# A float32 second product in column groups for a short last row block, in a mixture-of-experts kernel on one core

## The reference

```
top1 = argmax(softmax(x @ router_w + router_b))
for i in range(8):
    h = x @ w1[i] + b1[i]                 # 256 -> 2048
    a, g = split(h, 2)                    # 1024 each
    y = (a * sigmoid(g)) @ w2[i] + b2[i]  # 1024 -> 256
    out = out + where(top1 == i, y, 0)
out = x + out
```

## Time and profile before

| | us |
|---|---|
| median of 3 runs | 217.95 |
| profiled execution, time | 217.55 |
| profiled execution, span | 215.8 |
| prologue, to PE's first matmul of tile 0 | 38.8 |
| tiles 0 to 7 and the end | 177.0 |

### The profile page before, as it was taken

How to read it: one execution, slowest core, us unless ns; L and a number is a source line. 1 busy time by engine, 2 the same in 40 slices (tenths; PEclk the granted TensorE clock), 3 DMA queues, 4 the chain that set the end, 5 groups by cost and what they waited for, 6 DMA issues and landing times.

```text
span 215.8 us, 4313 instructions
## 1 busy us (share of the span) xinstructions
PE 205.6 (95%) x1500; PEld 191.2 (89%) x1502; DVE 159.1 (74%) x307; ACT 121.8 (56%) x204; POOL 124.6 (58%) x146
## 2 busy tenths in 40 slices
PE   6986998899999999999999999999999999999992
PEld 3756843799999999999999999999999999999991
DVE  6826984877835999298969879994898469874960
ACT  2333692365916666386684958483949185745620
POOL 5000038776730788558878787887487818730751
PEclk9999999999999999999999999999999999999998
DMA  4995523799757173976499559837835692720011
GB/s 140 368 402 186 219 82 91 257 274 380 220 131 307 46 234 71 314 196 204 109 289 288 186 114 362 295 91 184 355 114 180 178 313 70 248 49 0 24 39 36
DMA packets 16964, 41.26 MB, mean 191 GB/s; under 512 B 2856, under 2 KB 11177, under 8 KB 14762
## 3 DMA queue, kind: packets, MB, share of 16 engines
q1 hardware_dynamic: 11490, 28.32, 36.7%
q0 software_dynamic: 4512, 10.50, 19.4%
q10 hardware_dynamic: 936, 2.17, 2.6%
HBM read 36.78 MB, written 6.03 MB: 198 GB/s over the span
## 4 chain that ended last, share of the span: by engine, by line
PE 67%; POOL 14%; issue 8%; DVE 5%; DMA 3%; ACT 1%; DVEq 0%; ACTq 0%; POOLq 0%
PE y_ps L1049 7%; PE y_ps L1051 7%; PE y_ps L1050 7%; PE g_ps L1029 5%; PE g_ps L1034 5%; PE g_ps L1030 5%; POOL out_dram L384 5%; PE a_ps L1029 5%; PE a_ps L1034 5%; PE a_ps L1030 5%; POOL y_out L375 5%; PE y_ps L870 3%; PE y_ps L875 3%; DMA xg<-x_rows,g_idx 3%; POOL xg L363 3%
## 5 line engine op out<-in xcount | busy, mean ns | idle before, releaser
L384 POOL DMA_INDIRECT out_dram<-y_out,s_idx x30 | 44.0, 1466 | 41.2 <-DVE y_out L793 30.4
L524 ACT ACTIVATE arena<-g_ps,b_t 128x384 f32<-128x384 f32 (+1 forms) x64 | 34.4, 538 | 48.2 <-PE g_ps L1034 48.2
L766 DVE SCALAR_TENSOR_TENSOR arena<-a_ps,b_t,arena 128x384 f32<-128x384 f32 (+1 forms) x64 | 36.0, 563 | 30.9 <-PE a_ps L1034 28.4
L363 POOL DMA_INDIRECT xg<-x_rows,g_idx x32 | 37.1, 1159 | 37.1 <-DVE g_idx L732 26.5
L1049 PE MATMUL y_ps<-w_hi,u_hi 128*128 128x256 f32 x168 | 48.5, 289 | 0.1
L1050 PE MATMUL y_ps<-w_lo,u_hi 128*128 128x256 f32 x168 | 47.5, 283 | 0.0
L1051 PE MATMUL y_ps<-w_hi,u_lo 128*128 128x256 f32 x168 | 47.5, 283 | 0.0
L375 POOL DMA_INDIRECT y_out<-in_x_dram,g_idx x32 | 40.3, 1259 | 9.8 <-issue 9.8
L665 DVE TENSOR_TENSOR w_lo<-w_raw,w_hi 128x1024 fp32r<-128x1024 f32 x32 | 37.3, 1221 | 4.7 <-DMA xg<-x_rows,g_idx 3.0
L530 ACT ACTIVATE u_hi<-arena 128x384 fp32r<-128x384 f32 (+1 forms) x64 | 30.7, 480 | 16.0 <-DVE arena L766 16.0
L1029 PE MATMUL g_ps<-xr_hi,w_hi 128*128 128x256 f32 (+3 forms) x128 | 37.0, 303 | 0.6 <-ACT xr_hi L512 0.6
(11 more groups left out here) (150 smaller groups left out, 298.3 us busy)
## 6 DMA issues: line engine op xcount, KB each, us to landing
w_raw<-in_L_ffn_w_dram SPq DMA_DIRECT2D x16, 1024.0 KB, 8.9
w_raw<-in_L_ffn_w_dram SPq DMA_DIRECT2D x16, 512.0 KB, 5.0
arena<-in_x_dram SPq DMA_DIRECT2D x4, 512.0 KB, 6.2
x_rows<-arena ACTq DMA_DIRECT2D x4, 512.0 KB, 3.0
b_all<-in_L_ffn_b_dram SPq DMA_DIRECT2D x1, 1024.0 KB, 4.9
xg<-x_rows,g_idx POOLq DMA_INDIRECT x32, 7.1
y_out<-in_x_dram,g_idx POOLq DMA_INDIRECT x32, 4.5
out_dram<-y_out,s_idx POOLq DMA_INDIRECT x30
```

Source lines behind the costliest of these rows:

```text
L363: nc.gpsimd.indirect_dma_start(out=xg[:, s * DIM:(s + 1) * DIM], out_offset=None, in_=x_rows, in_offset=bass.IndirectOffsetOnAxis(ap=g_idx ...
L384: nc.gpsimd.indirect_dma_start(out=out_flat, out_offset=bass.IndirectOffsetOnAxis(ap=s_idx[:, i * NSUB + s:i * NSUB + s + 1], axis=0), in_ ...
L524: nc.scalar.activation(sig[:, c % SIG_RING, 0:n], pair[c % RING][1][:, 0:n], ACT.Sigmoid, bias=b1_t[:, bass.ds(e * (2 * NC) + (NC + c), 1) ...
L766: V.scalar_tensor_tensor(u32[:, c % (8 - SIG_RING), 0:n], pair[c % RING][0][:, 0:n], b1_t[:, bass.ds(e * (2 * NC) + c, 1)], sig[:, c % SIG ...
```

## The change

**PE.** For the sizes 192, 288 and 320 (`PARTS`: a last block of 32 or 64 tokens) the last block is computed by the new `part_block`: plain float32 matmuls from unsplit u (`u32`) and unsplit w2 (`w2_whole`), 64 or 32 columns of the array for one chunk, so that two or four chunks stand side by side in column groups that write to different partitions of `y_ps[1]`. Each group accumulates its own chunks. It waits for `pair_free` of each chunk and for `w2_whole`, in place of `u_lo`.

**DVE.** `add_parts` adds the partial sums of the groups above the first to the output rows: one addition of 64 partitions for 192 and 320, three of 32 for 288, in branches on the control word of the tile before.

**Widths.** The sizes are now 192, 256, 288, 320, 352, 512 (384 is gone, 192 is new; PE's first product still has at least 256 columns). ACT and DVE use widths of 256, 288, 320, 384 or 512 (`if_width`), a chain of branches over five bodies.

**Memory and loads.** `u32` holds all eight chunks and lies in `x_t`, which is free after the prologue. `w2_whole` takes the half of `arena` that `u32` had. SP loads it, 1 MB for each tile, after the next tile's w1 and when the second product of the tile before has ended.

With the given inputs tiles 0 (64 tokens over), 2 (64), 4 (32), 5 (32) and 7 (64) get a `part_block`; DVE's and ACT's widths fall from 384 to 320 in tile 0 and from 384 to 288 in tiles 4 and 5.

```diff
-    SIZES = (256, 288, 320, 352, 384, 512)
+    SIZES = (192, 256, 288, 320, 352, 512)
+    PARTS = {size: (size // P, size % P) for size in SIZES if size % P in (32, 64)}
...
+        def if_width(eng, word, body, low=0):
+            widths = (2 * P, 288, 320, 3 * P, ITEM)
+            firsts = (0, SIZES.index(288), SIZES.index(320), SIZES.index(352), SIZES.index(ITEM))
+            if low == len(widths) - 1:
+                body(widths[low])
+                return
+            with eng.If(f_size(word) < firsts[low + 1]):
+                body(widths[low])
+            with eng.Else():
+                if_width(eng, word, body, low + 1)
...
+            def load_w2_whole(e):
+                if e > 0:
+                    sp.wait_ge(w2_whole_loaded, 16 * e)
+                    sp.wait_ge(mm2_done, e)
+                sp.dma_start(w2_whole, w2[e].rearrange("(c p) d -> p c d", p=P)).then_inc(w2_whole_loaded, 16)
...
+            def add_parts(i, word, sizes_here):
+                def of_sizes(left):
+                    if not left:
+                        dve.sem_inc(dve_chain, more)
+                        return
+                    s, wide = PARTS[left[0]]
+                    with dve.If(f_size(word) == SIZES.index(left[0])):
+                        rows = y_out[i % YB][0:wide, s * DIM:(s + 1) * DIM]
+                        for g in range(1, P // wide):
+                            link(V.tensor_tensor(rows, y_ps[1][g * wide:(g + 1) * wide, PLACE[s] * DIM:(PLACE[s] + 1) * DIM],
+                                                 rows, ALU.add))
...
+                    with dve.Else():
+                        count[0] = start
+                        of_sizes(left[1:])
...
+            def part_block(size, at1, at2, at16, done=None):
+                s, wide = PARTS[size]
+                groups = P // wide
+                pe.wait_ge(w2_whole_loaded, at16)
+                for c in range(NC):
+                    pe.wait_ge(pair_free[c], at2 if c >= CARRIED else at1)
+                    g = c % groups
+                    last = T.matmul(y_ps[1][g * wide:(g + 1) * wide, PLACE[s] * DIM:(PLACE[s] + 1) * DIM],
+                                    u32[:, c, s * P:s * P + wide], w2_whole[:, c],
+                                    start=c < groups, stop=c >= NC - groups)
```

More of the change, by code:

```diff
@@ L261, in if_blocks, with word_registers @@
                     body(4)
+        def if_width(eng, word, body, low=0):
[8 more added lines that the diff above has]
+                if_width(eng, word, body, low + 1)
+        def word_registers(eng):
+            return [eng.alloc_register(f"word_at{a}") for a in range(2)]
         def word_register(eng, name):
@@ L552, in _ @@
             for e in range(NE):
[L553 removed]
+                if_width(act, this_word(act, word_at), lambda n: gate_tile(e, e, n))
             for i in range(NE, TAB):
@@ L785, in bank_rows, with add_rows, add_last @@
                 return rows[:, 1:3] if h else rows[:, 0:4:3]
-            def add_rows(i):
+            def add_parts(i, word, sizes_here):
[9 more added lines that the diff above has]
+                                                 rows, ALU.add))
+                        if P // wide - 1 < more:
+                            dve.sem_inc(dve_chain, more + 1 - P // wide)
+                    with dve.Else():
+                        count[0] = start
+                        of_sizes(left[1:])
+                start = count[0]
+                more = max(P // wide for _, wide in PARTS.values()) - 1
+                of_sizes(sizes_here)
+                count[0] = start + more
+            def add_rows(i, word):
                 dve.wait_ge(mm2_done, i + 1)
                 dve.wait_ge(b2_added, i + 1)
[L791 to L796, removed]
+                half = bank_rows(i, 0)
+                V.tensor_tensor(half, y_ps[0][:, :].rearrange("p (s d) -> p s d", s=2), half, ALU.add)\
+                    .then_inc(y_done[0], 1)
+                half = bank_rows(i, 1)
+                link(V.tensor_tensor(half, y_ps[1][:, :].rearrange("p (s d) -> p s d", s=2), half, ALU.add))
+                if word is not None:
+                    add_parts(i, word, list(PARTS))
+                dve.sem_inc(y_done[1], 1)
+            def add_last(i, blocks, n, word):
                 dve.wait_ge(b2_added, i + 1)
@@ L809, in add_last, with gate_tile @@
                     dve.sem_inc(y_done[h], 1)
-            def gate_tile(i, e, blocks):
-                n = blocks * P
+            def gate_tile(i, e, n, word=None, word_before=None, chain_at=None):
+                if chain_at is not None:
+                    count[0] = chain_at
+                blocks = -(-n // P)
                 split_x(i, n)
@@ L834, in gate_tile @@
                 if i == NE - 1:
-                    add_last(i, blocks)
+                    add_last(i, blocks, n, word)
             dve.wait_ge(x_rows_written, 4 * 16)
```

71 lines of the change are left out of this document (48 added, 23 removed).

## The result

The changed kernel takes **235.5 us** (median of 4, 232.3 to 237.4) where the kernel before takes 218.1; the ratio of the undisturbed runs is **1.069 (1.054 to 1.085)**. A second measurement gave 237.6 against 217.9, ratio 1.085 (1.078 to 1.092). The forecast was 224.4 (217.6 to 228.3): the direction was right, the size 11 us too small and outside the range.

The account below looks back on a forecast made before the run. PE, busy in 95% of the span, was taken as the bound. Its terms summed to +1.9 us and DVE's end added 4.6, so 217.55 became 224.0, by the median 224.4 (range 217.6 to 228.3).

Parts of the forecast that it names:

- the mechanism of code: On DVE and ACT: jumps over unused bodies cross instruction-block edges and wait 2.3 us for a fetch.
- the third wait: After DVE's last addition: three fetch waits of 2.3 us where there was one, the end +4.6 us.
- The sum on PE ... Total +1.9: Over PE's tiles: savings, load waits, jumps and late additions together cost 1.9 us, bounds -7 and +5.
- Matmuls, -7.2: PE's second product: part blocks save 1.1 us for each 64-token block, 1.95 for each 32-token block, 7.2 in all.
- w2_whole, +3.8: PE's part block waits for the second w2 load: 3.0 us in tile 4, 0.8 in tile 2.
- tiles 0, 5 and 7 have room: In these tiles the second w2 load comes in time; no wait was priced for it.
- The third rival: Gathers and code fetches share DMA with 8 MB more; loads land late in tiles 2, 4, 5: 228 us, 8%.
- Additions and late `gated`: DVE's additions at chunk 2 delay later work: +1.0 us in tile 5, +0.6 in tile 6, +0.3 in tile 7.
- Jumps: DVE and ACT between tile bodies: PE loses 0.8 us into tile 3, 1.0 into 4, 1.9 into 6.
- Fetches are rarer: Rival: larger blocks or fetching further ahead; middle nearly free of waits, end unchanged: 213.7 us, chance 15%.
- only the end suffers: Rival: one more fetch of 2.3 us at the end, w2_whole in time or PE even: 218 to 220.3, 15%.
- Two groups of 64 take turns: Rival in PE's part block: the column groups do not run side by side, three times 1.7 us more: 229, 5%.

Follow-up runs that it names:

- run 11: Kernel before with five bodies a tile on ScalarE and VectorE instead of three, at its old widths: 226.4 us, ratio 1.037.
- run 7: Changed kernel with the whole w2 loaded for the first expert alone, the seven later loads and their waits left out: 233.6 us, ratio 1.071.
- run 6: The changed kernel itself, unchanged, measured again on the chip of the kernel before: 237.6 us, ratio 1.085.
- run 13: Changed kernel with three bodies, second w2 load ahead of the next tile's w1, no load or part block for tile 0: 229.4 us, ratio 1.013.
- run 8: Kernel before plus only the second load of w2 of each expert, read by nobody: 222.7 us, ratio 1.018.
- run 2: Kernel before with one body for each tile on ScalarE and VectorE: 228.5 us, ratio 1.010.
- run 15: Kernel before with five bodies a tile on VectorE only, ScalarE keeping three: 229.0 us, ratio 1.014.
- run 17: Kernel before with the unread second w2 load, plus six filler matmuls ahead of TensorE's wait in the first tile: 230.1 us, ratio 1.022.
- run 18: Kernel before with the unread second w2 load, no filler, measured again: 227.8 us, ratio 1.010.
- run 16: Kernel before with five bodies a tile on ScalarE only: 226.2 us, ratio 1.001.
- run 4: Kernel before with five bodies a tile on ScalarE and VectorE, at its old widths, on a slower chip: 227.0 us, ratio 1.003.
- run 1: Changed kernel with one body for each tile on ScalarE and VectorE: 228.8 us, ratio 1.013.
- run 3: Changed kernel with three bodies for each tile on ScalarE and VectorE: 229.0 us, ratio 1.009.
- run 14: Changed kernel with three bodies a tile and VectorE's additions of partial sums left out: 227.8 us, no ratio because of scatter.

## Why the prediction was wrong

*The bound, the direction and the mechanism of code were right.* Jumps over unused bodies hold VectorE up at the starts of tiles 4 and 6. Priced together they came to 3.7 in the middle and 4.6 at the end, 8.3; run 11 has 8.7 for five bodies alone. That these are near each other is luck: in run 11's trace PE waits 3.8 in the middle, the clock behind it costs 1.7, the end has 2.2 more, and 1.4 more lie in the prologue. The division was wrong: the end got 2.1 more, for the third wait did not come, and the middle the rest. Each wait in the middle was priced at 2.3. Into tile 4 it is more: 3.7 in run 11, 4.2 in run 7, 6.0 in run 6 and the first. That instructions are fetched there is shown by their packets; that the fetch queues behind the weights is the reading, and shown is that the same jump, with as many packets, waits longer with more loads.

*The step that failed* is "The sum on PE ... Total +1.9", which became 15.4. Its terms, by the profile:

- *Matmuls, -7.2.* The time of the records was right to 0.2 a block of 32 and 0.3 of 64, 1.3 us in all. The tests that PE passes on its way to the right block were left out. In tile 7 nothing is late, and from the last matmul of the first product (220.56) to the first of the row blocks (223.46) it is 2.90, where before it took 0.12 and a block of 24 matmuls, 3.03. The block of 64 saved 0.1, not 1.1. Run 7 has the ways in bare, since no load is late there: 0.64 and 0.61 us in tiles 2 and 7, and 0.27 and 0.26 in tiles 4 and 5, where fewer tests are passed:

```profile
PE y_ps L1125 <- issue: 1.8, 4, 0.6
```

  In run 13, where two of the tests have a sum to work out first, they are 0.83, 0.95, 0.39 and 0.34. For all tiles of the first profile: a tile's length, less PE's idle time, less what the clock cost it (worked out below), fell by 6.3 us in the five tiles with a part block (104.9 to 98.6) and rose by 1.4 in tiles 1, 3 and 6 (67.6 to 69.0), for which I have no cause. Idle times beside which the trace has nothing but PE's own branches are 1.5 (0.2 ahead of tile 1, 0.4, 0.3 and 0.6 in tiles 3, 6 and 7). Together 3.4 us saved in place of 7.2, so 3.8 us of the error. The Trainium skill, "TensorEngine Tiling (Array Packing)", "Key Properties", says that a change of the mode drains the engine. The trace allows it about 0.1 us on entry: in tile 0 of run 7, with the tests passed while the transpositions ran, the first matmul in column groups starts 0.20 behind the last transposition (55.92, 56.12), where these follow each other at 0.11. So the 0.5 for all five that the prediction weighed and left out was about right, and was not the term that failed.
- *w2_whole, +3.8.* PE waited 3.9 for it, in other tiles (1.9 in tile 2, 0.6 in 4, 1.4 in 5). That the size came out is luck: by run 7, 1.2 of the 3.9 would have been PE's tests without any load. But the same bytes also made the gather of tile 1 late, priced at nothing since "tiles 0, 5 and 7 have room" looked only at who reads the load: 2.8 us. Run 8 shows it: nobody reads, 4.8 us lost. The third rival ("DMA is worse", 8%) named the gathers, in other tiles.
- *Nothing for the clock.* Every wait was priced at its own length. Behind those in tiles 0 and 2 the mean clock of the tile's window is 0.94 and 0.92, which is 0.06 x 27.85 + 0.08 x 21.68 = 3.4 us, beside 0.995 for the whole kernel before. Much of the scatter goes with it: in the second measurement's four runs and the first's the mean clock goes from 0.994 (232.3 us) to 0.959 (237.9). In run 6's profile tile 6 took 28.27 us, at a clock of 0.90 behind a wait of 3.1, where the first profile has 25.67 at 1.00 behind one of 2.9:

```profile
184.11:212.38 28.27, 27.84 (x172) 27.23 (x173) 22.70 (x32) 14.42 (x23) 9.97 (x8) 0.90 0.54 179
```

- *Additions and late `gated`*: 0.9 to 1.1 at three places, 3.0 in all, of which the prediction had 1.9 (tiles 5, 6 and 7).
- *Jumps*: 6.0 at tiles 4 and 6, where it had 3.7 for tiles 3, 4 and 6.

The errors sum to 3.8 + 2.8 + 3.4 + 1.1 + 2.3 = 13.4 of the 13.5 between +1.9 and +15.4; with the end's 2.5 the other way it is the 11 us of the total. The pieces run together rather than add: three bodies on the changed kernel give back 9 to 10, five cost the old one 8.7, and the load alone lengthens the jumps.

*The rivals.* "Fetches are rarer" and "only the end suffers" are out: the middle has most of it. "Two groups of 64 take turns" is out: 2.02 us for 64 against 1.02 for 32, as side by side gives.

## What to carry to other kernels

A wait of the busiest engine can cost more than its length, when the clock falls behind it: waits of 2.5 to 2.9 us cost 4.2 to 4.6 in tiles 0 and 2 here, while one of 3.2 cost no more than itself, and which it will be stays open. So look at the clock of the windows after it. Ask of an added transfer not only when its reader needs it, but which other transfers it delays. Code that is never executed has a price, which grows with what the queues carry: a body chosen at run time is paid for at each tile by the ones skipped. And count the tests on the busiest engine's own list: four in a row took 0.9 us here, most of it bare, ahead of a block that was to save 1.1.

## What was not expected of the hardware

- Two chips gave 217.7 to 217.9 us for the kernel before, two others 225.3 to 227.7. In profiles from the slower ones, of kernels made from the kernel before, PE issues only a few matmuls in some microseconds of tile 3 (runs 2, 15, 17 and 18, as shown for run 2) or of tile 4 (run 16), though not in run 4; in runs 1, 3, 13 and 14, made from the changed kernel, it doesn't. Open.
- The array's change to column groups is nearly free (0.1 us on entry in run 7). What costs is a test on PE's list, 0.2 us where its condition fails and 0.07 where it holds, once PE has caught up with its sequencer; a short product of 24 matmuls (2.9 us) hardly bears four of them.
- The same jump, into tile 4, kept VectorE for 4.2 us with one second load and for 6.0 with eight. The longest jumps with nearly idle queues, at the end, took 2.1 to 2.7.
